# A 1024-step GRU scan and a top-2 expert layer on one core: thirty-two more steps projected up front, logits of eight columns, a reordered last part

## The reference

```python
# x: (4, 1024, 1024), the start state: (4, 1024), W_ih and W_hh: (1024, 3072), float32
def cell(h, x):                               # scanned over 1024 steps of x
    gi = x @ W_ih + b_ih
    gh = h @ W_hh + b_hh
    r = sigmoid(i_r + h_r); z = sigmoid(i_z + h_z)
    n = tanh(i_n + r * h_n)
    h_new = (1 - z) * n + z * h
# every state h of every step (4096 rows of 1024) then goes through 8 experts, top 2 of them:
logits = h / max(norm(h), 1e-12) @ router_w                   # 8 columns
combine = softmax(logits), its two largest, scaled to sum 1
out = sum_e combine[:, e] * (h @ Wa[e] @ Wb[e])               # rank 128
return x + out
```

## Time and profile before

| | us |
|---|---|
| median of three runs | 9643.99 |
| the profiled execution's own time | 9650.36 |
| its span | 9648.6 |
| PE busy | 9574.9 (99%) |
| DVE busy | 5882.6 (61%) |
| ACT busy | 1209.9 (13%) |
| up front, until PE's first matmul of step 0 | 140.43 |
| the last part, from PE's last matmul of the scan to the span's end | 75.7 |

### The profile page before, as it was taken

How to read it: one execution, slowest core, us unless ns; L and a number is a source line. 1 busy time by engine, 2 the same in 40 slices (tenths; PEclk the granted TensorE clock), 3 DMA queues, 4 the chain that set the end, 5 groups by cost and what they waited for, 6 DMA issues and landing times.

```text
span 9648.6 us, 543874 instructions
## 1 busy us (share of the span) xinstructions
PE 9574.9 (99%) x246424; PEld 7573.1 (78%) x246424; DVE 5882.6 (61%) x30339; ACT 1209.9 (13%) x4955; POOL 491.5 (5%) x1142
## 2 busy tenths in 40 slices
PE   7999999999999999999999999999999999999999
PEld 4568887888787888878888878888788778888676
DVE  5666666666666666566666666656665566656664
ACT  2111111111111111111111111111111111111111
POOL 1000000000000000000000000000000000000100
PEclk9999999999999999999999999999999999999999
DMA  7232222222222223333333333333333333333343
GB/s 191 81 91 63 62 69 61 65 60 65 66 61 67 59 64 83 80 80 78 76 82 81 80 76 75 83 81 79 82 74 82 79 82 80 76 78 79 87 99 90
DMA packets 1208078, 759.53 MB, mean 79 GB/s; under 512 B 850224, under 2 KB 996144, under 8 KB 1205744
## 3 DMA queue, kind: packets, MB, share of 16 engines
q1 hardware_dynamic: 1181424, 646.76, 27.1%
q0 software_dynamic: 24336, 77.98, 3.6%
HBM read 566.37 MB, written 184.88 MB: 78 GB/s over the span
## 4 chain that ended last, share of the span: by engine, by line
PE 97%; SPq 1%; DMA 1%; DVE 0%; issue 0%; ACT 0%; DVEq 0%
PE gh_ps L1360 82%; PE gi_ps L1429 11%; PE y_ps L1469 1%; PE y_ps L1482 1%; PE gi_ps L1382 1%; SPq L420 1%; PE route_ps L1442 1%; DMA projection<-in_L_cond_W_ih 1%; PE gi_ps L1400 0%; PE gh_ps L1560 0%; PE gi_ps L1469 0%; PE gi_ps L1482 0%; DMA projection<-w_ih_by_partition 0%; PE gi_ps L1546 0%; PE route_ps L1400 0%
## 5 line engine op out<-in xcount | busy, mean ns | idle before, releaser
L1360 PE MATMUL gh_ps<-w_hh_parts,h_parts 128*12 128x288 bf16 (+1 forms) x196608 | 8424.2, 326 | 11.2 <-DVE h_parts L1010 7.5
L1360 PEld LDWEIGHTS gh_ps<-w_hh_parts,h_parts 128*12 128x12 bf16 x196608 | 6097.0, 88 | 1719.3 <-issue 91.0
L959 DVE STREAM_TRANSPOSE gh<-gh_ps 128x288 f32<-128x288 f32 (+1 forms) x2048 | 1197.1, 585 | 2156.4 <-PE gh_ps L1360 2117.2
L1429 PE MATMUL gi_ps<-projection 128*32 128x128 f32 x37632 | 1411.1, 273 | 3.4 <-DMA projection<-w_ih_by_partition 3.3
L1429 PEld LDWEIGHTS gi_ps<-projection 128*32 128x32 f32 x37632 | 1209.4, 110 | 190.2 <-DMA projection<-w_ih_by_partition 4.9
L1276 ACT ACTIVATE gate<-pre 128x24 f32<-128x24 f32 (+1 forms) x2048 | 473.5, 231 | 6963.0 <-DVE pre L972 6963.0
L965 DVE TENSOR_REDUCE gh_sum<-gh 128x36 f32<-128x108 f32 (+1 forms) x2048 | 652.6, 319 | 71.1
L980 DVE TENSOR_TENSOR h_cand<-h_cand,gate 128x12 f32<-128x12 f32 (+1 forms) x2048 | 361.2, 176 | 436.7 <-ACT gate L1276 436.2
L1279 ACT ACTIVATE cand<-h_cand 128x12 f32<-128x12 f32 (+1 forms) x2048 | 445.4, 217 | 932.7 <-DVE h_cand L983 932.7
L992 DVE TENSOR_TENSOR zn<-one_minus_z,cand 128x12 f32<-128x12 f32 (+1 forms) x2048 | 360.1, 176 | 249.6 <-ACT cand L1279 7.2
L1005 DVE TENSOR_TENSOR h_parts<-shared,h_parts 128x12 bf16<-128x12 f32 (+1 forms) x2048 | 359.9, 176 | 217.9 <-DVE shared L1000 6.7
(11 more groups left out here) (167 smaller groups left out, 2474.7 us busy)
## 6 DMA issues: line engine op xcount, KB each, us to landing
projection<-w_ih_sums SPq DMA_DIRECT2D x672, 256.0 KB, 3.1
projection<-w_ih_by_partition SPq DMA_DIRECT2D x504, 256.0 KB, 2.8
gi<-gi_scratch SPq DMA_DIRECT2D x256, 192.0 KB
gi_scratch<-gi_stage SPq DMA_DIRECT2D x360, 128.0 KB, 2.4
shared<-wa_by_partition SPq DMA_DIRECT2D x58, 512.0 KB, 4.7
expert_b<-in_L_ffn_Wb SPq DMA_DIRECT2D x58, 512.0 KB
x_raw<-expert_rows_of_h SPq DMA_DIRECT2D x228, 128.0 KB
projection<-in_L_cond_W_ih SPq DMA_DIRECT2D x192, 128.0 KB, 3.6
```

What stands on the lines that cost most here:

```text
L959: nc.vector.transpose(gh[k][:, :, :, :], ps[k][sp_][:, 0:GATES * n * Q].rearrange("p (q c i) -> p q c i", q=GATES, i=Q))\
L1360: ins = nc.tensor.matmul(ps[k_out][t % 2][j * Q:j * Q + SPLIT * B, 0:GATES * (o1 - o0) * Q], h_parts[:, (t - 1) % 2, c, :, :].rearrange("p ...
L1429: ins = nc.tensor.matmul(ps_i[(pair + BANK[s]) % 2][j * Q:(j + 1) * Q, 0:COLS // 2], w_half[q % WH][:, c, j * Q:(j + 1) * Q], x_of[what][: ...
```

## The change

1. **Up front.** `project_wide` takes one chunk of 1024 output columns (512 KB, one DMA, rows of 4 KB) in place of two chunks of 512, with two buffers in place of three. Each of the 24 loads now serves 32 matmuls with 256 moving columns (block 0) and 32 with 128 moving columns: the first 32 steps of block 1 (`x_ahead`). Block 0's sums go to the four banks of the recurrence, two columns in a bank, those of block 1 to `ps_i`. ACT evicts at three points (after pieces 10, 21 and 32 of W_hh), 16 activations each. For block 0's first two chunks of four steps, ACT writes gi itself (`turn_first`), with no trip through DRAM. `load_x` issues 8 DMAs in place of 16. The blank lists are written before W_hh is loaded, and the copy of W_a by partition moves from the start to block 2.
2. **Block 0.** `project` has 128 moving columns (steps 32 to 63 of block 1) in place of 256, still 192 tiles.
3. **Router.** In 31 of 33 windows `logits` loads the 8 router columns and moves the window's 32 columns; DVE turns the result back (`rank`), and ACT makes the sums of squares from the rows (`square`, two activations of 512 columns). The tables move by a step to make room. The last two windows keep the old form (`logits_and_gram`).
4. **Last part.** The first two experts' products with the window that is complete stand before the wait for the last h; the others take both windows in one matmul of 256 moving columns in place of two of 128; expert 3's stands behind the scale matmuls.

```diff
-AT_RECORD = {5: 0, 37: 1}
-AT_WEIGHT = {4: 0, 36: 1}
+AT_RECORD = {6: 0, 38: 1}
+AT_WEIGHT = {5: 0, 37: 1}
+AT_SQUARE = {5: 0, 37: 1}
...
-    WR = 3
+    WIDE = 2
+    GC = 2 * NQ
+    HALF_COLS = COLS // 2
...
+        ahead_rows = [late[:, at_last:at_last + FB], late[:, at_last:at_last + FB], wide[0]]
...
-        first_banks = [ps_i[0], ps_i[1], ps_r, ps_y]
+        first_banks = [ps[k][s] for k in range(2) for s in range(2)]
...
             def load_wide(i):
-                g, c = i // 4, i % 4 * 2 * Q
-                for j in range(NQ):
-                    sp.dma_start(wide[i % WR][j * Q:(j + 1) * Q, :, :],
-                                 w_ih[j * GW + c:j * GW + c + 2 * Q, g * 4 * P:(g + 1) * 4 * P]
-                                 .rearrange("(c i) n -> i c n", i=Q)).then_inc(w_i_in[i % WR], DMA)
+                g, c = i // NC, i % NC
+                sp.dma_start(wide[i % WIDE], w_ih[:, g * GC * P:(g + 1) * GC * P]
+                             .rearrange("(j c i) n -> c j i n", j=NQ, i=Q)[c, :, :, :]).then_inc(wide_in[i % WIDE], DMA)
...
+                if m % NC == 1 and m > NC:
+                    for h in range(2):
+                        store_first(m // NC * 2 - 2 + h)
+                    store_ahead(m // NC - 1)
+            for h in range(2):
+                store_first(NM // 4 - 2 + h)
+            store_ahead(GATES - 1)
+            sp.wait_ge(first_out, DMA * 3 * GATES)
+            load_w(1, 1, WL)
...
+                    if n == 2 and t % 4 == 2 and t < 4 * (E + 1):
+                        copy_a(t // 4)
...
+            def turn_first(h):
+                if h == 0:
+                    act.wait_ge(lists_clear, DMA)
+                act.wait_ge(gi_read, 4 * (h + 1))
+                here = first_rows[h % 2].rearrange("p (c t b) -> p c t b", c=4, b=B)
+                for s in range(2):
+                    nc.scalar.activation(gi[s][:, h // 2, h % 2 * 4:h % 2 * 4 + 4, :, :],
+                                         here[:, :, s * CH:(s + 1) * CH, :], ACT.Copy).then_inc(first_turned, 1)
...
+                for g in range(GATES):
+                    if n == PIECES * (g + 1) // GATES:
+                        if g:
+                            act.wait_ge(first_out, DMA * 3 * g)
+                            act.wait_ge(first_turned, 4 * g)
+                        else:
+                            act.wait_ge(ahead_ready, NC)
+                        for k in range(GC * g, GC * (g + 1)):
                             evict_first(k)
+                        evict_ahead(g)
+                        for h in (2 * g, 2 * g + 1):
+                            turn_first(h)
...
             def project_wide(i):
-                g, c0 = i // 4, i % 4 * 2
+                g, c = i // NC, i % NC
+                pe.wait_ge(wide_in[i % WIDE], (i // WIDE + 1) * DMA)
...
+                for k in range(GC):
+                    if c == 0 and g:
+                        pe.wait_ge(gi_read, (g - 1) * GC + k // 2 * 2 + 2)
+                    for j in range(NQ):
+                        ins = nc.tensor.matmul(
+                            first_banks[k // 2][j * Q:(j + 1) * Q, k % 2 * COLS:(k % 2 + 1) * COLS],
+                            wide[i % WIDE][:, k * P + j * Q:k * P + (j + 1) * Q],
+                            x_t[:, c, :, :].rearrange("p t b -> p (t b)"), ...)
...
+                for k in range(GC):
+                    if c == 0 and g and k % 4 == 0:
+                        pe.wait_ge(ahead_read, (g - 1) * GC + k + 4)
+                    for j in range(NQ):
+                        ins = nc.tensor.matmul(
+                            ps_i[k // 4][j * Q:(j + 1) * Q, k % 4 * HALF_COLS:(k % 4 + 1) * HALF_COLS],
+                            wide[i % WIDE][:, k * P + j * Q:k * P + (j + 1) * Q],
+                            x_ahead[:, c, :, :].rearrange("p t b -> p (t b)"), ...)
...
             def logits(v, half):
+                if v:
+                    pe.wait_ge(sq_done, 2 * v)
+                for c in range(NC):
+                    for b in range(B):
+                        ins = nc.tensor.matmul(ps_r[b * Q:b * Q + E, 0:Q], rw[:, c, :],
+                                               window_at[half][:, :, c, b], start=(c == 0), stop=(c == NC - 1))
...
+            def square(v):
+                act.wait_ge(nat_in, DMA * (v + 1))
+                act.wait_ge(pos_ready, v + (START + 1))
...
+                    nc.scalar.activation(ps_r[:, :], nat[:, h * HALF:(h + 1) * HALF], ACT.Square,
+                                         accum_out=squares[h]).then_inc(sq_done, 1)
...
             for i in range(NM):
                 project_wide(i)
-            pe.wait_ge(cleared, 4)
+            pe.wait_ge(gi_read, NM)
...
+            pe.wait_ge(y_ready, 2 * DONE + START)
+            for e in range(2):
+                late_hidden(e, (0,))
+            for k in range(2):
+                pe.wait_ge(parts_ready[k], T + 1)
+            pe.wait_ge(taken_ready, 2 * NB)
+            logits_and_gram(0)
...
-            for e in range(4):
-                late_hidden(e)
+            for e in range(3):
+                late_hidden(e, (1,) if e < 2 else (0, 1))
...
+            late_hidden(3, (0, 1))
```

More of the change, by code:

```diff
@@ L288, in recurrence @@
         xt_ready = sem("xt_ready")
-        w_i_in = [sem(f"w_ih_in{s}") for s in range(WR)]
+        wide_in = [sem(f"w_ih_rows_in{s}") for s in range(WIDE)]
+        w_i_in = [sem(f"w_ih_in{s}") for s in range(WL)]
         w_half_in = [sem(f"w_half_in{s}") for s in range(WH)]
@@ L526, in _ @@
             load_x(0)
[L527 removed]
+            for m in range(WIDE):
                 load_wide(m)
+            load_half_x(0, ahead_raw, ahead_in)
             sp.wait_ge(rows_cleared, 1)
@@ L695, in _ @@
                 .then_inc(lists_clear, DMA)
+            for n in range(PIECES):
+                if n >= RAW:
+                    pool.wait_ge(w_high, n - RAW + 1)
+                    pool.wait_ge(w_rest_ready, n - RAW + 1)
+                pool.dma_start(w_raw[n % RAW], piece(w_hh, n)).then_inc(w_in[n % RAW], DMA)
             def count_up(tile, pattern, base, step):
@@ L1174, in steps @@
                     if t in AT_RANK:
-                        rank(n * 2 + AT_RANK[t], AT_RANK[t])
+                        rank(n * 2 + AT_RANK[t], AT_RANK[t], 0, last and AT_RANK[t] == 1)
                     if t in AT_POS and not (last and AT_POS[t]):
@@ L1324, in steps @@
                         copy_product(f, q)
+                    if t in AT_SQUARE and not (last and AT_SQUARE[t]):
+                        square(n * 2 + AT_SQUARE[t])
                     if t in AT_RECORD:
@@ L1512, in steps @@
                     if t in AT_LOGITS:
-                        logits(n * 2 + AT_LOGITS[t], AT_LOGITS[t])
+                        if last and AT_LOGITS[t]:
+                            pe.wait_ge(sq_done, 2 * (n * 2 + AT_LOGITS[t]))
+                            logits_and_gram(AT_LOGITS[t])
+                        else:
+                            logits(n * 2 + AT_LOGITS[t], AT_LOGITS[t])
                     if t in AT_PLACE and not (last and AT_PLACE[t]):
@@ L1529, in _, with late_hidden @@
             steps(NB - 1, True, True)
-            for k in range(2):
-                pe.wait_ge(parts_ready[k], T + 1)
-            pe.wait_ge(taken_ready, 2 * NB)
-            logits(2 * NB, 0)
-            pe.wait_ge(y_ready, 2 * DONE + START)
-            def late_hidden(e):
-                pe.wait_ge(z_wa_in[e], DMA)
+            def late_hidden(e, windows):
+                bank = z_banks[e % 4]
+                if windows != (1,):
+                    pe.wait_ge(z_wa_in[e], DMA)
                 if e == 3:
```

239 lines of the change are left out of this document (144 added, 95 removed).

## The result

| | before | after |
|---|---|---|
| median of 4 runs, us | 9644.72 | 9700.5 (9697.05 to 9709.99) |
| span of the profiled execution, us | 9648.6 | 9695.1 |
| first matmul of step 0 | 140.43 | 244.22 |
| block 0, first matmul to block 1's | 595.2 | 552.5 |
| blocks 1 to 15, sum | | 6.2 less |

The ratio is 1.0063, interval 1.0051 to 1.0076: slower by 0.63%, where 0.54% faster was forecast and 9622 us was the upper end of the range. The times of the scan's matmuls, read from the timelines, give the whole difference of the spans: +103.8 up front, -42.7 in block 0, -6.2 in the other blocks, -8.4 at the end make +46.5, which is 9695.1 - 9648.6.

What follows compares the result with a forecast made beforehand. PE, busy for 99% of the span, was taken as the bound. From 9650.36 us, -41.3 - 7.4 + 15.3 - 11.6 - 6.7 = -51.7 gave 9598.7; with the median 6.4 lower, 9592, range 9553 to 9622.

Steps and rivals of the forecast that it cites:

- C: Up front: wider W_ih loads, landing in 6.2 us on average, start the scan later, +15.3 us; ends +3 and +47.
- The sign that I had set for C: Up front: PE waits for `wide_in` of over 40 us in sum behind the first would prove C wrong.
- The loads become the bound outright: Rival up front: loads of 13 us make PE wait in `project_wide`, C is +97, time 9674 us; chance 0.04.
- As slow as the lone one of 8.8: Rival up front: loads stay at 8.8 us, C is +47, time 9624 us; chance 0.12.
- A: Block 0: tiles half as wide take 41.3 us off PE; other end -28.5.
- the chain-bound rival: Rival in block 0: narrower tiles don't shorten its steps; A is -28.5, time 9605 us; no chance of its own.
- the 10 that would have proved A wrong: Block 0: PE waits for h_parts of over 10 us would prove A wrong.
- B: First step: the 4.89 us wait for gi and 2.51 us of the slow A half go, -7.4 us; other end 0.
- D: Logits in 31 windows: moving 32 columns for 40 cuts a call from 1.87 to 1.50 us, -11.6; ends 0 and -44.6.
- The cheap-logits rival: Rival in the logits: loaded columns set the pace, a call takes 0.43 us, D is -44.6, time 9559; chance 0.17.
- E: Last part: early products and fewer instructions fill waits and gaps, -3.4, -1.3 and -1.9, together -6.7 us; ends -3 and -8.6.
- F: Work moved at no cost (copy of W_a into block 2, scatters a step later): 0; other end +5 us.

Runs made afterwards that it cites:

- e1: The changed kernel with each 512 KB load of W_ih up front as four DMAs of 32 partitions; 9635.06 us, ratio 0.9996.
- e5: The kernel before, with each W_ih load's four DMAs of 128 KB cut with the four groups outermost; 9702.49 us, ratio 1.0062.
- e4: The changed kernel with the edits of e1 and e3 together; 9611.78 us, ratio 0.9969.
- e8: e4 with at most two pieces of W_hh in flight in place of four; 9607.5 us, ratio 0.9964.
- e9: e8 with a group's three 512 KB stores up front each behind another W_ih load, not all behind one; 9602.88 us, ratio 0.9962.
- e6: e4 with the logits in the old form in all 33 windows; 9631.89 us, ratio 0.9989.
- e7: e4 with the logits moving 32 adjacent columns (other data than the window's); 9598.08 us, ratio 0.9956.
- e10: e8 with the last part in the order of the kernel before, keeping the 256-column matmuls; 9606.72 us, ratio 0.9965.
- e3: The changed kernel with only the loads of x rewritten, 32 steps outermost in place of four groups; 9678.37 us, ratio 1.0039.

## Why the prediction was wrong

**C, up front, is the step that failed.** It priced a load's landing by "one DMA takes a quarter, which leaves 6.6", counted wider rows in its favour, and took 6.2. This saw a DMA as bytes and an issue, and never asked over how many engines it is spread. With nothing but W_ih being loaded, a load takes 8.7; the four-way form costs 65 us in this kernel (e1) and 57 in the kernel before (e5). I had +15.3, at most +47; measured +103.8. The sign that I had set for C came: the waits behind the first are 87.5 - 27.5 = 60.0 us, over 40. The 8.8 us that the 6.2 was worked out from was not of a lone load either: behind it, from 29.03 on, SP's queue in the kernel before took the sixteen DMAs of x. Its parts:

- The first load lands at 27.5 for 20.2 (+7.3).
- 24 turns of 6.94 would be 167 us and end at 194.
- The other 50 us lie in the stretches with more in the queues. The first two turns, 14.2 and 14.9 us, are 15 of them, with one wait of 5.8 us for x and the longest one for a load, 8.4 at 56.58. Of the rest, the turns that end and begin at 143.90 took 12.7 and 10.4 us, the first of them beside stores and W_hh. From 120 to 140 the granted clock was 0.77, behind a stretch in which PE had waited, and the matmuls (64 records) that take 3.66 us took 6.05: PE loses there by waiting and by the slower clock.

With both mended the start is 173.3, with W_hh held back 164.3, where the forecast had 155.7. Of e4's 18 us over the forecast 4 to 9 are W_hh's bursts (e8), none the stores (e9); the rest stays open.

**The rivals.** "The loads become the bound outright" named the right place, the wait of `project_wide`, and a time of 9674, and had 4%. Its reason was a crowded queue at 13 us a load. What speaks against it is the share of 0.25 in the stretches without W_hh: there was no crowd, and PE waited. "As slow as the lone one of 8.8" had the right duration by accident (8.7), with the engines "full" as its reason. The trace of before could only show full engines, as its loads were spread. The code showed the rest: the outermost dimension of both forms stood in the diff.

The bound of a quarter of the engines could have been priced: 276 / 4 = 69 GB/s by the earlier trace rows, an estimate of 7.6 us for 512 KB with nothing beside it, a turn of (5.17 + 7.6)/2 = 6.4. The rule of the Trainium skill that the prediction weighed (DMA: Bandwidth & Descriptors, Queues, rings and completion order), turns between queues by packet, says nothing of a load that is alone, and no run here tests it (the prediction's working took a packet for one row; in the trace of before W_hh's packets are of 6 KB, two rows); the one that mattered, on the number of engines, stands on the same page.

**A, block 0: right in kind, 7 us short.** -42.7 with step 0 and two windows' logits in it, against -41.3, -7.4 and -0.7. A step is 8.53 in the median (9.10 before), 0.57 less and not 0.65. The missing part stands in the slot with one tile: it takes 515.28 - 514.99 = 0.29 us, where half of the 0.43 before would be 0.215, and now and then there is a wait for the second part of h besides:

```profile
506.16 0.39 PE L1489 MATMUL gi_ps<-projection 128*32 128x128 f32 x8
506.75 5.05 PE L1470 MATMUL gh_ps<-w_hh_parts,h_parts 128*12 128x288 bf16 x120 [0.19 <-DVE h_parts L1067]
...
514.99 0.39 PE L1489 MATMUL gi_ps<-projection 128*32 128x128 f32 x8
515.28 5.05 PE L1470 MATMUL gh_ps<-w_hh_parts,h_parts 128*12 128x288 bf16 x120
```

That is the edge to the chain-bound rival (-28.5), which is passed only now and then: PE's waits for h_parts in block 0 are 1.5 us in sum, far from the 10 that would have proved A wrong. What the 0.07 us of the other steps is the trace doesn't name.

**B, the first step: right.** No wait for gi; the first two steps are 6.2 and 3.1 shorter, 9.3 for -7.4 and A's share of two steps, -1.3.

**D, logits: right sign, the size too small.** 20, not 11.6 (e6). From its first to its last record a call came down from 1.77 us to 1.20 in the median of the 31 (1.04 to 1.30), a factor of 0.68 and not 0.80. The distance of the moved columns is about half of what a call costs (e7), so it matters, as I took it, but scaling by their number (32 for 40) was too careful. By their line (ns, min/median/max) the median record takes 267 with 32 moved columns at 128 bytes, and 315 with 40, a factor of 0.85; yet the call is shorter than that. Which of the other differences between the two forms gives the rest (8 loaded columns for 32 is one) was not tried apart:

```profile
L1565 PE MATMUL route_ps<-shared,router x1984: 216/267/313, 252.5 to 9048.1; 128*8 128x32 f32 x199
```

The cheap-logits rival had a call at 0.43 us with the moved columns left at their distance; it is at 1.2, and e7 gets to 0.56 only by moving adjacent ones, so that rival is out. The rule of the Trainium skill, SBUF — State Buffer (Door 1: The DMA port swizzle), on lines of 16 bytes points the same way.

**E, the last part: right.** -8.4 against -6.7, of which the new order is 3.1 (e10) and not 4.7. With the old order the last part is still 5.1 shorter than before (70.6 for 75.7); that this comes from half as many matmuls for the last experts was not tried alone. The wait of 3.50 is gone; of the gaps two of about 1 us are left:

```profile
9619.85 7.96 PE gh_ps L1470 x192
9627.81 3.50 PE gi_ps L1676 x127
...
9631.33 2.11 PE route_ps L1573 x55
...
9634.95 1.11 issue
...
9641.25 1.02 issue
```

**F, moved at no cost: wrong by 11.** The copy of W_a shows no cost. The load of x does: step 57 of 13 blocks stands 15.5 us over 9.11 in sum, where it was 4.7 before, and e3 takes all of it away. I had listed it as eight DMAs fewer to issue, and so as a gain.

In sum, with C's and F's fault mended the forecast was near: e4 has 9611.8 and e9 9602.9 where 9592 was predicted. Part of that is luck: the logits gave 9 us more than forecast, which about covers the 7 that block 0 gave less, so that e4's miss looks like C's 18 alone.

## What to carry to other kernels

Fewer and larger DMAs are no gain by themselves: read the outermost dimension of both sides of each rewritten transfer. The runs here tried 4 and 32; for what lies between there is only the rule of the Trainium skill quoted above, by which a multiple of 16 gives all the engines. While PE waits for a load, the DMA share of that stretch helps to tell the cases apart, if it is read slice by slice and beside what was issued: 1.00 was bandwidth here (276 GB/s), a steady quarter was how the transfer was cut, and a mean over mixed slices says neither (0.73 in e1, 0.23 in e5). And a load that nobody waits for can still hold back a small one behind it on the same engines, so the price of a rewritten transfer is looked for at its neighbours too.

## What the runs showed of the hardware

- SP loads of 512 KB with an outermost dimension of 4 ran at a DMA share of 0.24 and 75 GB/s with nothing beside them (0.25 and 87 beside x, written alike), and one took 8.7 us. The same bytes in four DMAs with 32 outermost let PE work without a wait at 5.20 us a load.
- Two such DMAs in place of one stayed on a quarter (share 0.27, 100 GB/s) and gained 13 us of the 65.
- Rows of 1 KB on a quarter of the engines (95 GB/s, e5) went no slower than rows of 4 KB (75 to 87).
- A load of 256 KB queued behind 1 MB with an outermost dimension of 4 came late for PE in 13 blocks, 15.5 us in sum; with 32 outermost in none.
- 32 float32 matmuls that move 32 columns at a distance of 128 bytes took 1.17 us from first to last record, with adjacent columns 0.56 (medians of 31 calls).
- With 8 loaded columns, four column groups and 32 adjacent moved columns the matmul records started 8.4 ns apart on average (0.54 us / 64 records, two to a float32 matmul).
